# First attention of a two-layer gated block: operand stacks made on chip instead of through DRAM

## The reference, cut to what matters

```python
q = (x @ Wq.T + bq).reshape(B, N, H, D).transpose(0, 2, 1, 3)
kv = (y @ Wkv.T + bkv).reshape(B, M, 2, H, D).transpose(2, 0, 3, 1, 4)
k, v = (kv[0], kv[1])
q = _layernorm(q, q_gamma, q_beta) * SCALE          # over the 8 dimensions of a head
k = _layernorm(k, k_gamma, k_beta)
attn = jax.nn.softmax(jnp.einsum('bhnd,bhmd->bhnm', q, k), axis=-1)
out = jnp.einsum('bhnm,bhmd->bhnd', attn, v)
out = out.transpose(0, 2, 1, 3).reshape(B, N, C)
return out @ Wproj.T + bproj
# the caller: x = x + jnp.tanh(g_xattn[0]) * that, with x layer-normalised going in
```

## Time and profile before

| | |
|---|---|
| median of three runs | 964.08 us |
| profiled execution | 962.42 us |
| its span | 960.7 us |
| TensorE busy | 790.6 us, 82% |
| VectorE busy | 570.4 us, 59% |
| ScalarE busy | 348.4 us, 36% |
| POOL busy | 255.3 us, 27% |
| mean granted clock of TensorE | 0.865 |

### The profile page before, as it was taken

One profiled execution on the slowest core, in us unless ns is written; L12 is line 12 of the kernel. 1 busy time (PEld: TensorE's weight loads), 2 busy tenths in 40 slices (PEclk: granted clock), 3 DMA queues, 4 the chain that ended last, 5 costly groups with the idle time before them and its releaser, 6 DMA issues.

```text
span 960.7 us, 13961 instructions
## 1 busy us (share of the span) xinstructions
PE 790.6 (82%) x5494; PEld 548.7 (57%) x5494; DVE 570.4 (59%) x1212; ACT 348.4 (36%) x506; POOL 255.3 (27%) x160
## 2 busy tenths in 40 slices
PE   5275359999996889987999799988999784998896
PEld 4252124444445677764766567666767552777685
DVE  5544224454526887866867777777766766254343
ACT  3242123454452333362454344433544431302200
POOL 3245000000000001053555345554564644001100
PEclk9675556676777999998999999998999988899998
DMA  5264640000004000300000000000000000000000
GB/s 130 38 114 78 123 74 2 1 0 1 2 1 175 1 1 1 88 1 1 1 2 2 1 1 2 1 1 1 2 1 2 1 1 1 1 6 1 5 6 6
DMA packets 37041, 21.02 MB, mean 22 GB/s; under 512 B 12504, under 2 KB 35688, under 8 KB 36848
## 3 DMA queue, kind: packets, MB, share of 16 engines
q1 hardware_dynamic: 36976, 20.13, 9.9%
HBM read 17.14 MB, written 2.88 MB: 21 GB/s over the span
## 4 chain that ended last, share of the span: by engine, by line
PE 60%; DVE 19%; SPq 6%; issue 6%; DMA 4%; ACT 3%; POOL 1%; POOLq 0%; ACTq 0%; DVEq 0%
PE ps L1435 59%; SPq L449 3%; DVE mx L1024 3%; DVE rs_t L907 2%; DVE o L1244 2%; DMA scr<-parts 2%; DMA kq<-mrow 1%; DVE pmax L1228 1%; ACT v L575 1%; SPq L427 1%; DVE stats L922 1%; DVE rs_y L918 1%; PE ps L1446 1%; DVE ysum L1345 1%; SPq L445 1%
## 5 line engine op out<-in xcount | busy, mean ns | idle before, releaser
L1435 PE MATMUL ps<-p,v 128*64 128x256 f32 (+1 forms) x1280 | 154.8, 474 | 18.5 <-ACT mrow L575 15.0
L786 ACT ACTIVATE p<-ps 128x1024 f32<-128x1024 f32 x96 | 96.4, 1026 | 135.1 <-PE ps L1435 135.1
L1024 DVE TENSOR_REDUCE mx<-ps 128x1 bf16<-128x512 f32 x128 | 81.7, 687 | 103.9 <-PE ps L1435 92.9
L1435 PE MATMUL ps<-kqh 64*128 64x256 f32 (+1 forms) x640 | 107.2, 369 | 41.8 <-DVE pmax L1228 32.4
L1435 PEld LDWEIGHTS ps<-p,v 128*64 128x64 f32 (+1 forms) x1280 | 73.5, 149 | 84.9 <-issue 37.1
L549 POOL TENSOR_TENSOR acc<-p 128x1024 f32<-128x1024 f32 x32 | 75.8, 2369 | 124.8 <-ACT p L786 124.8
L552 POOL TENSOR_TENSOR acc<-acc,p 128x1024 f32<-128x1024 f32 x32 | 76.0, 2375 | 109.7 <-ACT p L786 109.7
L1435 PEld LDWEIGHTS ps<-kqh 64*128 64x128 f32 x640 | 60.1, 194 | 67.5 <-DVE pmax L1228 35.2
L1228 DVE TENSOR_REDUCE pmax<-ps 128x2 f32<-128x1024 f32 x64 | 78.3, 1223 | 28.4 <-PE ps L1435 26.7
L673 ACT ACTIVATE p<-ps 128x1024 f32<-128x1024 f32 x64 | 65.1, 1024 | 74.3 <-PE ps L1435 54.9
L1435 PE MATMUL ps<-kr,qmr 32*128 32x512 f32 x128 | 63.2, 596 | 12.6 <-DVE mx L1024 11.4
(11 more groups left out here) (249 smaller groups left out, 1452.4 us busy)
## 6 DMA issues: line engine op xcount, KB each, us to landing
kq<-scr SPq DMA_DIRECT2D x12, 384.0 KB
scr<-parts SPq DMA_DIRECT2D x12, 192.0 KB, 2.9
kq<-scr SPq DMA_DIRECT2D x36, 64.0 KB
w<-in_L_ffn_W_dram SPq DMA_DIRECT2D x1, 2048.0 KB, 12.0
wt<-in_L_ffn_W_dram SPq DMA_DIRECT2D x4, 512.0 KB, 6.6
ctx_all<-in_ctx_dram SPq DMA_DIRECT2D x4, 256.0 KB, 3.1
raw_kv<-in_L_xattn_Wkv_dram SPq DMA_DIRECT2D x1, 1024.0 KB, 5.0
raw<-in_L_ffn_B_dram SPq DMA_DIRECT2D x9, 64.0 KB
```

The costliest lines, as they stand in the source:

```text
L786: act.activation(p1[:, g % 2, u, :], bank(2 * (n % 2), 2), ACT.Exp, scale=SCALE1).then_inc(a_exp1.sem, 1)
L1024: dve.tensor_reduce(mx0[:, q % 2, n % 2, n // 2:n // 2 + 1], bank(4 + m % 3), AX, ALU.max).then_inc(d_max0.sem, 1)
L1435: return pe.matmul(o, lhsT, rhs, start=start, stop=stop)
```

## The change

The stacks are made by TensorE. `prep_final` writes a high half `kfh` (rounded to fp32r) and the full value; POOL subtracts and gives the low half `kfl`. A constant matrix `emat` of zeros and ones picks, for quad v, the 8 rows of four heads out of 128 and writes them at three slots of a 32-row block for each head: keys high, high, low (`stack_k`), queries high, low, high (`stack_q`). ScalarE copies both to SBUF; the bias column `onecol` puts a one in row 24 of the key stack. POOL makes four copies of the query stack in `q4`, each with all but one head's 32 rows set to zero by `rmask`. Maxima and scores then both use all 128 rows of `kst` and `q4`, in fp32r, and the row of maxima goes to row 24 of `q4` as fp32.

What is taken away: `scr`, `parts`, `kq`, `kr`, `qmr`, `mk4`, `onesrow` and all of their transfers. What else is moved: the small bias loads go to ScalarE's queue; the loads of all tokens stand first; the four batches are normalised together, the roots in two pairs; centring is a step of its own behind the squares; the raw weights are turned in one PSUM bank (6) instead of two, with the spreads of batches 0 and 1 and value projections of 2 and 3 between them; the maxima have two banks (4, 5) instead of three; `p0` has 8 buffers instead of 7. The stack of quad q+3 is made in round q.

```diff
-                sp.wait_ge(s_part.sem, s_part.after(b, 48))
-                if b == 3:
-                    sp.wait_ge(e_wT.sem, WT_GROUPS)
-                if b >= 2:
-                    sp.dma_start(kq[SR:SR + 1, b, :, 0:NC_], onesrow[0:H, :]).then_inc(s_ones[b - 1].sem, 16)
-                w = NPART * D0
-                for m in range(NPART):
-                    sp.dma_start(kq[m * w:(m + 1) * w, b, :, 0:NC_],
-                                 scr[b].rearrange("h s d n -> (s d) h n")[:, :, 0:NC_]).then_inc(s_kq[b].sem, 16)
-                    for s in range(NPART):
-                        at = m * w + s * D0
-                        sp.dma_start(kq[at:at + D0, b, :, NC_:NK],
-                                     scr[b][:, m, :, NC_:NK].rearrange("h d n -> d h n")).then_inc(s_kq[b].sem, 16)
 
             def maxima_row(q):
-                b, v = divmod(q, NQUAD)
                 sp.wait_ge(a_rows0.sem, q + 1)
-                sp.dma_start(kq[SR:SR + 1, b, v:H:NQUAD, NC_:NK], mrow0[:, q % 2, :]).then_inc(s_mrow.sem, 16)
-
-            stacked(0)
-            stacked(1)
...
-            pool.memset(onesrow[:, :], 1.0).then_inc(g_ones.sem, 1)
+            pool.memset(emat[:, :, :, :].bitcast(F32), 0.0).then_inc(g_emat.sem, 1)
+            pool.wait_ge(g_emat.sem, 1)
+            turned = ident[:, :].rearrange("p (r v d) -> p v r d", r=QUAD, v=NQUAD)
+            for kind, slot in ((0, 0), (0, 1), (1, 2), (2, 0), (2, 2), (3, 1)):
+                to = emat[:, kind, :, :].rearrange("p v (r s d) -> p v r s d", r=QUAD, s=4)[:, :, :, slot, :]
+                pool.tensor_copy(to, turned).then_inc(g_emat.sem, 1)
             pool.memset(onesb[:, :], 1.0)
...
                 for v in range(QUAD):
-                    ins = pool.tensor_scalar(qmr[:, b, v, :], kf[:, k, NC_:NK], mk4[:, v:v + 1], None, ALU.mult)
-                ins.then_inc(g_qm.sem, 1)
-                pool.wait_ge(g_r1.sem, b + 1)
-                pool.wait_ge(a_p1.sem, b + 1)
-                pool.tensor_tensor(parts[:, k, 2, :], kqc[:, k, :], parts[:, k, 1, :],
-                                   ALU.subtract).then_inc(g_p2.sem, 1)
+                    pool.tensor_scalar(q4[:, q % SLOTS, v, :], qst[:, q % 2, :], rmask[:, v:v + 1], None,
+                                       ALU.mult).then_inc(g_q4.sem, 1)
...
+            def prep_centred(b):
+                k = b % 2
+                o = bank(3 * k + (2 if b < 2 else 0))
+                at = slice(b // 2 * NQ, (b // 2 + 1) * NQ)
+                ident_of(kqc[:, b, 0:NC_], o, bcols[:, 1:2])
+                ident_of(kqc[:, b, NC_:NK], bank(3 * k + 1)[:, at], bcols[:, 0:1]).then_inc(a_kqc.sem, 1)
+
             def prep_final(b):
-                k = b % 2
                 act.wait_ge(d_kn.sem, d_kn.after(b, 2))
                 if b >= 2:
-                    act.wait_ge(g_p2.sem, b - 1)
-                    act.wait_ge(s_part.sem, s_part.after(b - 1, 0))
-                ident_of(kf[:, k, 0:NC_], kqc[:, k, 0:NC_], gcols[:, 1:2], gcols[:, 0:1])
-                ident_of(kf[:, k, NC_:NK], kqc[:, k, NC_:NK], gcols[:, 5:6], gcols[:, 4:5]).then_inc(a_kf.sem, 1)
-                act.wait_ge(a_kf.sem, b + 1)
-                copy(parts[:, k, 0, :], kf[:, k, :]).then_inc(a_p0.sem, 1)
-                copy(kr[:, b, :], kf[:, k, 0:NC_]).then_inc(a_kr.sem, 1)
-
...
+            prep_context(1)
+            prep_tokens(0)
+            prep_tokens(1)
             prep_squares(0)
             prep_squares(1)
-            prep_final(0)
-            prep_final(1)
-            prep_turned(2)
-            prep_turned(3)
-            prep_middle(0)
-            prep_middle(1)
+            prep_context(2)
+            prep_context(3)
+            prep_centred(0)
+            prep_centred(1)
             prep_squares(2)
             prep_squares(3)
+            prep_centred(2)
+            prep_centred(3)
             for n in range(WT_GROUPS - 2):
                 wt_group(n)
-            prep_final(2)
-            prep_final(3)
-            prep_middle(2)
-            prep_middle(3)
             act.wait_ge(s_small.sem, 16 * (SMALL_LOADS + 1))
             act.activation(gates[:, :], gates_raw[:, :], ACT.Tanh).then_inc(a_tanh.sem, 1)
...
+            def stack_q(q):
+                act.wait_ge(e_qst.sem, q + 1)
+                if q >= 2:
+                    act.wait_ge(g_q4.sem, g_q4.after(q - 1, 0))
+                copy(qst[:, q % 2, :], bank(Q_BANK[q])[:, 0:NQ]).then_inc(a_qst.sem, 1)
+
+            def stack_k(q):
+                act.wait_ge(e_kst.sem, q + 1)
+                if q >= SLOTS:
+                    act.wait_ge(e_st0.sem, e_st0.after(q - SLOTS + 1, 0))
+                ident_of(kst[:, q % SLOTS, :], bank(K_BANK[q]), onecol).then_inc(a_kst.sem, 1)
+
+            stack_q(0)
+            stack_k(0)
+            stack_q(1)
+            stack_k(1)
+            stack_k(2)
+            stack_q(2)
             rows_out(0)
             for q in range(AQ + 1):
                 turning = q >= NQUAD + 1 and q % NQUAD == 1
+                ahead = q + SLOTS - 1 < AQ
                 if q < AQ:
                     exp0(4 * q)
                     if q + 1 < AQ:
                         rows_out(q + 1)
+                    if ahead:
+                        stack_q(q + SLOTS - 1)
                     exp0(4 * q + 1)
                     if turning:
                         oT_out(q // NQUAD - 1)
-                        exp0(4 * q + 2)
+                    if ahead:
+                        stack_k(q + SLOTS - 1)
+                    exp0(4 * q + 2)
+                    if q >= 1:
                         o0_out(q - 1)
-                    else:
-                        if q >= 1:
-                            o0_out(q - 1)
-                        exp0(4 * q + 2)
...
+                pe.wait_ge(a_wT.sem, n + 2)
                 for m in range(4 * n, min(4 * n + 4, NT)):
-                    ins = pe.transpose(tok(bank(6 + n % 2), m % 4), raw[:, m, :], ident[:, :])
+                    ins = pe.transpose(tok(bank(6), m % 4), raw[:, m, :], ident[:, :])
                 if n == WT_GROUPS - 3:
-                    ins = pe.transpose(bank(6 + n % 2)[:, 3 * P:3 * P + E], gate0_raw[:, :], ident[0:E, 0:E])
+                    ins = pe.transpose(bank(6)[:, 3 * P:3 * P + E], gate0_raw[:, :], ident[0:E, 0:E])
                 ins.then_inc(e_wT.sem, 1)
+                if n < 2:
+                    prep_spread(n)
+                    context_values0(n + 2)
             prep_spread(2)
             prep_spread(3)
 
+            def stack_mm(o, hi, lo, kind, v):
+                mm(o, emat[:, kind, v, :], hi, True, False)
...
+            def stack_q(q):
+                b, v = divmod(q, NQUAD)
+                if v == 0:
+                    pe.wait_ge(g_kfl.sem, b + 1)
+                if q >= SLOTS - 1:
+                    pe.wait_ge(a_kst.sem, q)
+                    pe.wait_ge(a_qst.sem, q)
+                stack_mm(bank(Q_BANK[q])[:, 0:NQ], kfh[:, b, NC_:NK], kfl[:, b, NC_:NK], 2, v).then_inc(e_qst.sem, 1)
+
+            def stack_k(q):
+                b, v = divmod(q, NQUAD)
+                if K_BANK[q] == Q_BANK[q]:
+                    pe.wait_ge(a_qst.sem, q + 1)
+                stack_mm(bank(K_BANK[q]), kfh[:, b, 0:NC_], kfl[:, b, 0:NC_], 0, v).then_inc(e_kst.sem, 1)
 
             def row_max0(q, n):
                 m = 8 * q + n
-                b, v = divmod(q, NQUAD)
                 r, t = divmod(n, 2)
-                if n == 0 and v == 0:
-                    pe.wait_ge(a_kr.sem, b + 1)
-                    pe.wait_ge(g_qm.sem, b + 1)
-                if m >= 3:
-                    pe.wait_ge(d_max0.sem, m - 2)
-                at = slice(32 * r, 32 * r + 32)
-                mm(bank(4 + m % 3), qmr[at, b, v, t * P:(t + 1) * P], kr[at, b, :]).then_inc(e_max0.sem, 1)
+                if n == 0:
+                    pe.wait_ge(a_kst.sem, q + 1)
+                if t == 0:
+                    pe.wait_ge(g_q4.sem, g_q4.after(q, r + 1))
+                if m >= 2:
+                    pe.wait_ge(d_max0.sem, m - 1)
+                mm(bank(4 + m % 2), q4[:, q % SLOTS, r, t * P:(t + 1) * P],
+                   kst[:, q % SLOTS, :]).then_inc(e_max0.sem, 1)
 
...
             def scores0(n):
                 q, r = divmod(n, QUAD)
-                b, v = divmod(q, NQUAD)
-                h = NQUAD * r + v
                 if r == 0:
-                    if v == 0:
-                        pe.wait_ge(s_kq[b].sem, 192)
-                        pe.wait_ge(s_ones[max(b - 1, 0)].sem, 16)
                     pe.wait_ge(s_mrow.sem, s_mrow.after(q, 16))
                 if n >= 2:
                     pe.wait_ge(a_exp0.sem, n - 1)
                 for k in range(TC):
-                    ins = mm(bank(2 * (n % 2), 2)[:, k * NQ:(k + 1) * NQ], kq[0:SR + 1, b, h, k * P:(k + 1) * P],
-                             kq[0:SR + 1, b, h, NC_:NK])
```

(42 more changed lines are left out.)

328 lines of the change are left out of this document (176 added, 152 removed).

## The result

The changed kernel takes 889.31 us (median of four runs, 887.67 to 893.82) against 962.73 us (four runs, 960.42 to 964.66): a ratio of 0.925 with a 95% interval of 0.920 to 0.929. The forecast was 890 us. The profiled execution took 890.85 us, with a span of 889.1 us against 960.7 us.

What follows compares the result with a forecast made beforehand. DMA queueing, then TensorE's low clock, were taken to bound the first attention. Start 72.7, loop 133.6 and tail 11.5 us end it at 217.8, 74.2 us earlier: 888.2 us profiled, 890 us median, range 868 to 932 us.

Steps and rivals of the forecast that it cites:

- The bound: First attention: a 46.6 us stall from queued DMA issues, then a loop bound by TensorE at mean clock 0.70.
- The clock: First attention's loop: granted clock 1.00 instead of 0.70, as almost every product fills 128 rows; otherwise 45 us more.
- Rival A: Loop's clock stays as before, adding 3 us to each of 15 rounds: 935 us; chance 0.20 including states between.
- Rival C: Clock at 1.2 GHz right through the loop, 14.6 us a round, about 975 us, slower than before; chance 0.04.
- Rival B: Another engine's order, ScalarE's stack copies between exponentials, adds a 1 us wait per round: 10 us rounds, 906 us; chance 0.16.
- The round: One loop pass over four heads: 7.1 us of products plus waits, 8.9 us at the full clock.
- Its idle: In each round TensorE waits about 1.2 us, after the third scores, for ScalarE's exponential and copy of `o`.
- The 0.12 us: In the loop: four scores take 0.48 us as full-array products instead of 0.60 us, without a change of tiling mode.
- the seam: Between rounds: with two banks for maxima, the pair there waits twice for VectorE's reductions, 0.6 us.
- The rounds with a turned batch: Three of the loop's rounds, each costing about 1.5 us more than 8.9 us.
- The start: Everything before the loop: first scores at about 72.7 us instead of 91.6 us.
- The tail: From the last scores to the end of the first attention: 11.5 us, kept from the earlier trace.

Runs made afterwards that it cites:

- experiment 6: Kernel before the change, with only the rows of maxima sent from ScalarE's DMA queue instead of SyncE's; 944.97 us, ratio 0.985.
- experiments 1 to 4: Changed kernel with fewer rows in products: maxima from 32 rows 945.69 us; scores from 32, 947.78; both from 32, 967.50; maxima from 64, 906.82.
- experiment 1: Changed kernel with the products for the maxima read from 32 rows instead of 128; 945.69 us, ratio 0.984 to the kernel before.
- experiment 4: Changed kernel with the products for the maxima read from 64 rows instead of 128; 906.82 us, ratio 0.946 to the kernel before.
- experiment 3: Changed kernel with the products for both maxima and scores read from 32 rows instead of 128; 967.50 us, ratio 1.005 to the kernel before.
- experiments 2 to 4: Changed kernel with scores from 32 rows, 947.78 us; maxima and scores from 32 rows, 967.50 us; maxima from 64 rows, 906.82 us.
- Experiment 5: Changed kernel with ScalarE copying `o` ahead of the third exponential, except in rounds that turn a batch; 885.27 us, ratio 0.922 to the kernel before.
- the second group: Later group of runs, all on one chip, in which the unaltered changed kernel was measured again; 895.79 us, ratio 0.929 to the kernel before.

## Why the prediction was right, step by step

- **The bound.** Right in both halves: a queue of DMA issues, and a clock. Of the 29.2 us won where the stall was, experiment 6 gets 17.9 by queue order alone.
- **The clock.** Chosen as 1.00, measured 1.00 from 89.6 to 205 us. The reason given, that almost every product fills 128 rows, is what experiments 1 to 4 bear out, with one correction: maxima from 64 rows kept it too from 100 us on, though it came later. What in a 32-row product costs the clock they don't say. With both products at 32 rows the changed kernel is as slow as the one before (967.5 against 961.4 us), though start and stall are won. The clock is thus not one term of the gain but its condition. The Trainium skill's "TensorE: Matmul & The Clock Gate", in its part on oscillation in real kernels, names idle gaps as what takes the clock away; here it was at 1.2 GHz from 131.5 to 134.5 us of experiment 1 with TensorE busy for 3.00 of 3.00 us, so the measurement differs from that rule. The fall at 139 to 140 us came behind a wait of 0.73 us; the changed kernel has one of 0.92 us in each round and keeps its clock.
- **Rival A** was priced too low. I added 3 us to a round by the mean clock of 0.70; with 32-row maxima the mean was 0.69 to 0.71 and a round 13.8 us, 4.8 more. About 0.6 of that is the switch, as in experiment 4. The rest is more than the mean says, since much of the time at the high level holds a wait (136.0 to 138.0 us: busy for 1.53 of 2.00) and the low level falls on dense products. The price is 52 to 57 us (by ratio, against the two measurements of the changed kernel; 53.0 and 54.4 by the attention's end) and not 45; it isn't 15 times 4.8 because some rounds kept more of the clock (from 168.88 to 178.94 us a round took 10.1). **Rival C** (14.6 us a round, 975 us) did not happen here, but experiment 3 lies near it, at a loop clock of 0.62 where I had put the turning point at 0.55. **Rival B** was not seen: the round above has no other wait of about 1 us.
- **The round.** 8.9 us predicted, 8.99 measured. Its idle was put at 1.2 us and is 0.92. The terms written for it don't give 1.2: with the 0.65 us of the scores they add up to 1.63, without them, as the scores are no idle time, to 0.98, and that is nearly what was measured. The 0.12 us by which four scores were to get shorter is hardly there: behind the `p,v` group it took 0.60 us from scores to maxima in the earlier trace rows and takes 0.58 now. So the rows compared there are no evidence of what a switch costs; experiments 2 to 4 are. As to the rest, the seam was put at 0.6 us and shows as 0.18 us of wait for VectorE, while products run slower than the back-to-back figures (a pair of maxima 0.63 us in the round). The rounds with a turned batch cost 0.9 us more, not 1.5. From the first scores to those of the last quad it makes 133.3 us for 133.6: thirteen rounds 0.09 us too short in the forecast and three turned batches 0.6 us too dear nearly cancel.
- **The start.** 74.7 us against 72.7 for the first scores. TensorE's first products came at 9.78 us, not 8; the weights' turning then went faster (1.3 us a group, not 1.7, until the clock fell), and was over at 48.5 us (49). The last subtraction ended at 60.1 (61.2). The 2 us came behind it: at the low clock the maxima of the first two quads take 1.64 us a pair, products and reductions in turn, and not the 1.2 us of VectorE alone (the rows are TensorE's first products, then a group of turned weights, the last subtraction and the first maxima).

```profile
9.78 1.20 PE L1442 MATMUL ps<-cen,raw 128*128 128x128 f32 x4 [9.78 <-DMA raw<-in_L_xattn_Wproj_dram]
```

```profile
42.36 0.66 PE L1546 MATMUL ps<-ident,raw 128*128 128x128 f32 x4 [0.69 <-ACT wt L544]
58.33 1.80 POOL L492 TENSOR_TENSOR kfl<-kf,kfh 128x768 fp32r<-128x768 f32 x1 [0.61 <-ACT kf L547]
61.18 1.19 PE L1442 MATMUL ps<-kst,q 128*128 128x512 f32 x2 [3.88 <-POOL q L499]
```

- **The tail** is the term that was mis-sized: 15.1 us from the first scores of the last quad, at 208.0 us, to the end of the attention, where I kept the 11.5 us of the earlier trace rows. I had counted ScalarE's new order in every round but not in the tail. There it costs 0.7 us between these scores and the next `p,v` group (2.0 us against 1.4) and 1.5 us from that group to its turned `o` (4.0 against 2.4), and the last group fell at the low clock, 1.4 us:

```profile
213.97 0.44 PE L1623 MATMUL ps<-ident,o 128*128 128x128 f32 x2 [1.39 <-ACT o L544]
215.99 3.34 PE L1442 MATMUL ps<-p,v 128*32 128x256 f32 x32 [1.11 <-ACT p L648]
```

Experiment 5 shows it. With the copy ahead of the exponential the same tail takes 11.8 us (198.61 to 210.38), there is no wait ahead of that turned `o`, and the last group has the full clock:

```profile
202.55 0.43 PE L1627 MATMUL ps<-ident,o 128*128 128x128 f32 x2
204.73 1.93 PE L1446 MATMUL ps<-p,v 128*32 128x256 f32 x32 [1.28 <-ACT p L648]
```

- **The sum.** The attention ended at 223.1 us, 5.3 us later than forecast: 2.0 of the start, 3.6 of the tail, 0.3 less in between. The later stages, expected at 668 to 669 us, took 666.0 in that execution and 675.3 in the other. So it took 890.85 us where 888.2 was forecast, and the median then lay 1.5 us below it where I had added 1.7. That 889.3 came so near to 890 is luck: with later stages as long as before it would have been some 3 us more, and the same program had a median of 895.8 us in the second group.

## What to carry to other kernels

A product that fills few rows of the array is not cheap where it stands in a dense stream: look at the granted clock of the stretch, and if it is low while TensorE is busy, try the same sums over more rows, with zeros in the rest. When a queue's order causes a stall, price a move to another queue by itself before rebuilding the data's path. And when a stage is edited, read the gain from the point in the trace at which that stage ends: stages behind it can move by more than the edit is worth.

## What was not expected of the hardware

- Full clock with little useful data: products over 128 rows of which 96 are zeros in one operand ran at a clock of 1.00 for 115 us, and at 0.99 in experiment 5 with TensorE busy for 94% of the loop; with 32 of the same rows named, 0.65 to 0.82 in one window and 0.62 to 0.75 over the loop.
- The later stages of one unchanged piece of program took 665.5 to 666.0 us (three profiles), 668.4 to 668.7 (four) and 672.2 to 675.5 (five), in good part by the granted clock of the second attention (0.95 to 0.97 in its middle in the first seven, 0.93 in four of the last five; experiment 1 had 0.97 and took 672.2 us all the same). What decides it in an execution stays open; the changed kernel has both with starts only 1.3 us apart (223.1 and 221.8 us).
